# Neighbourhood attention on one core: the denominators' transfers move from SyncE's queue to ScalarE's, the division and the output projection to later tiles, and the queries' split parts to earlier ones

## The reference, cut to what matters

```
x = x + attention(group_norm(x))

qkv = (x @ w_qkv + b_qkv) -> q, k, v        # 16 heads of 8 channels
for each of the 7 x 7 neighbours (a, b) of a position:
    logit = sum_d(q * k[neighbour]) + rpb[head, offset]
attn = softmax over the 49 neighbours
out  = sum over neighbours of attn * v[neighbour]
return out @ w_proj + b_proj
```

## Time and profile before

| | before |
|---|---|
| median of 3 runs | 1369.31 us (1366.49 to 1371.41) |
| profiled execution | 1369.89 us, of which 1368.1 us from the first to the last instruction |
| PE busy | 1142.9 us, 84% of the span |
| DVE busy | 896.4 us, 66% |
| ACT busy | 672.9 us, 49% |
| POOL busy | 580.8 us, 42% |
| mean granted clock of TensorE | 0.868 of full speed |

### The profile page before, as it was taken

The page is one execution under the profiler, slowest core; times in us unless marked ns, Lnnn a source line. Parts: engine busy times, 40 slices in busy tenths (PEclk is TensorE's granted clock), DMA queues, the critical chain, the costliest instruction groups (busy, mean ns, idle before and its releaser), DMA issues.

```text
span 1368.1 us, 33536 instructions
## 1 busy us (share of the span) xinstructions
PE 1142.9 (84%) x12441; PEld 781.8 (57%) x12441; DVE 896.4 (66%) x2136; ACT 672.9 (49%) x1867; POOL 580.8 (42%) x1278
## 2 busy tenths in 40 slices
PE   3799999564889898988889898989888898989883
PEld 3555555362556565655556566656556565656561
DVE  2422222497778686877778686868677686868672
ACT  2200000420657566575657566666656575665761
POOL 3000000410446473746556464737455464637361
PEclk7699999755789899998888999989998888999996
DMA  9200000060574746656574746456565747465562
GB/s 256 57 36 36 36 35 36 24 157 13 120 160 116 147 115 133 149 105 166 118 172 112 163 109 140 130 118 148 116 167 128 158 107 161 112 136 146 105 161 52
DMA packets 142458, 159.17 MB, mean 116 GB/s; under 512 B 29952, under 2 KB 119888, under 8 KB 142040
## 3 DMA queue, kind: packets, MB, share of 16 engines
q1 hardware_dynamic: 141432, 153.13, 48.6%
q0 software_dynamic: 864, 3.90, 0.9%
HBM read 86.09 MB, written 70.47 MB: 114 GB/s over the span
## 4 chain that ended last, share of the span: by engine, by line
PE 50%; DMA 20%; DVE 12%; SPq 9%; issue 6%; ACT 1%; POOL 1%; POOLq 0%; DVEq 0%; ACTq 0%
PE PS L1088 14%; PE PS L1194 9%; DMA area<-q_parts 8%; DMA sums<-packed 8%; PE PS L1157 8%; SPq L436 5%; PE PS L1178 4%; PE PS L1204 4%; PE PS L1100 4%; DVE bias L941 3%; PE PS L1171 3%; PE PS L1141 3%; DVE area L983 3%; DMA area<-x 2%; SPq L488 1%
## 5 line engine op out<-in xcount | busy, mean ns | idle before, releaser
L578 POOL TENSOR_TENSOR halves<-masked 128x96 f32<-128x96 f32 (+1 forms) x512 | 202.8, 396 | 445.7 <-DVE masked L1015 405.9
L1194 PE MATMUL PS<-S,VT 128*36 128x96 f32 (+1 forms) x4096 | 295.2, 270 | 9.9 <-ACT S L761 9.9
L761 ACT ACTIVATE S<-S 128x384 f32<-128x384 f32 (+1 forms) x512 | 270.0, 538 | 64.8 <-DVE S L1004 64.2
L1004 DVE TENSOR_TENSOR S<-PS,bias 128x384 f32<-128x384 f32 (+1 forms) x513 | 283.1, 552 | 7.6 <-PE PS L1157 7.5
L754 ACT ACTIVATE VT<-PS 128x128 f32<-128x128 f32 x449 | 125.9, 280 | 329.2 <-PE PS L1141 323.6
L1157 PE MATMUL PS<-area 97*128 97x48 bf16 (+1 forms) x4112 | 257.1, 210 | 31.7 <-DMA area<-q_parts 22.2
L1194 PEld LDWEIGHTS PS<-S,VT 128*36 128x36 f32 x4096 | 178.5, 120 | 155.1 <-issue 94.5
L1157 PEld LDWEIGHTS PS<-area 97*128 97x128 bf16 x4112 | 185.7, 104 | 118.9 <-DMA area<-q_parts 26.2
L994 DVE TENSOR_REDUCE mcol<-PS 128x6 bf16<-128x480 f32 (+2 forms) x297 | 181.1, 610 | 89.5 <-PE PS L1178 88.0
L1015 DVE TENSOR_TENSOR masked<-PS,cst 128x192 f32<-128x192 f32 (+1 forms) x512 | 181.3, 354 | 85.7 <-PE PS L1194 80.1
L1088 PE MATMUL PS<-area 128*128 128x392 f32 x576 | 192.9, 498 | 3.8 <-DVE area L883 3.8
(11 more groups left out here) (87 smaller groups left out, 1130.2 us busy)
## 6 DMA issues: line engine op xcount, KB each, us to landing
k_parts<-area SPq DMA_DIRECT2D x204, 168.0 KB, 3.0
area<-k_parts SPq DMA_DIRECT2D x33, 1008.0 KB, 7.6
q_parts<-area SPq DMA_DIRECT2D x204, 98.0 KB, 2.2
area<-q_parts SPq DMA_DIRECT2D x66, 294.0 KB, 8.1
xa<-x_mid SPq DMA_DIRECT2D x18, 392.0 KB, 4.8
late<-x_mid SPq DMA_DIRECT2D x17, 392.0 KB, 7.2
out<-area SPq DMA_DIRECT2D x17, 392.0 KB, 6.2
den<-sums SPq DMA_DIRECT2D x66, 98.0 KB
```

The costliest lines, as they stand in the source:

```text
L578: nc.gpsimd.tensor_tensor(h, m[:, :, 0:2, :], m[:, :, 2:4, :], ALU.add).then_inc(s["half"], 1)
L761: nc.scalar.activation(S[:, n % 4, 0:cols], S[:, n % 4, 0:cols], ACT.Exp).then_inc(s["probs"], 1)
L1004: nc.vector.tensor_tensor(S[:, n % 4, 0:cols], PS[:, SCORE + n % 2, 0:cols], bias[:, at:at + cols], ALU.add).then_inc(s["biased"], 1)
L1194: last = mm(PS[64 * (g % 2):64 * (g % 2) + VALUE_COLS, SUM + n % 2, at:at + q], VT[:, w % 4, g, :], S[:, n % 4, q * g:q * (g + 1)], start= ...
```

## The change

Five things are changed, all in the loop.

1. The six transfers of the denominators are issued by ACT, not SP, at fixed steps: `sums<-late` at step 3, `packed<-sums` at step 5, `sums<-packed` at step 8, `den<-sums` at step 11, each at the end of ACT's step with the wait that SP had ahead of it.
2. The reciprocals move from DVE's step 6 to 7, behind that step's maxima, and the division from step 12 to 14.
3. Both halves of the projection are at PE's step 15, one behind the other. ACT keeps the result at step 15 as before.
4. ACT writes the queries' second part at step 11 of the even chunk, not 14. POOL writes their third part at steps 14 and 15, not 17 and 18 (1 and 2 of the odd chunk).
5. SP's queue loses the six transfers and their waits, and keeps the order of the rest.

```diff
-        MISC_PROJECT, MISC_TURN = 13, 24
+        MISC_PROJECT, MISC_TURN = 15, 24
...
-        FIRST_BANK, RECIPROCAL, NORMALIZE, NEXT_IMAGE, RESIDUAL = 1, 6, 12, 30, 20
+        FIRST_BANK, RECIPROCAL, NORMALIZE, NEXT_IMAGE, RESIDUAL = 1, 7, 14, 30, 20
+        COLLECT, PACK, SPREAD_OUT = 3, 5, 11
...
-        SECOND = {8: ("k", 0), 10: ("k", 1), 14: ("q", 0)}
+        SECOND = {8: ("k", 0), 10: ("k", 1), 11: ("q", 0)}
...
-        THIRD = {10: ("k", 0), 11: ("k", 1), 12: ("k", 2), 13: ("k", 3), 17: ("q", 0), 18: ("q", 1)}
+        THIRD = {10: ("k", 0), 11: ("k", 1), 12: ("k", 2), 13: ("k", 3), 14: ("q", 0), 15: ("q", 1)}
...
                         store_keys(j, i + 1, True)
-                        collect_denominators(j, c)
                         store_queries(j, i + 1, True)
                         fill_keys(j, c + 1)
-                        spread_reciprocals(j, c)
                         fill_queries(j, c + 1)
...
+                        if n == COLLECT:
+                            collect_denominators(j, c)
+                        if n == PACK:
+                            pack_denominators(j, c)
+                        if n == RECIPROCAL + 1:
+                            store_reciprocals(j, c)
+                        if n == SPREAD_OUT:
+                            spread_reciprocals(j, c)
...
-                        if MISC_PROJECT <= n < MISC_PROJECT + 2:
-                            project_out(j, c, n - MISC_PROJECT)
+                        if n == MISC_PROJECT:
+                            for g in range(2):
+                                project_out(j, c, g)
```

52 lines of the change are left out of this document (28 added, 24 removed).

## The result

| | before | after |
|---|---|---|
| median of 3 runs | 1369.31 us | 1429.99 us (1429.94 to 1437.98) |
| ratio to before | | 1.0446 (95% interval 1.0415 to 1.0476) |
| span of the profiled execution | 1368.1 us | 1428.2 us |
| PE busy, PE idle (span less busy) | 1142.9, 225.2 us | 1170.4, 257.8 us |
| mean granted clock | 0.868 | 0.865 |

The changed kernel takes 60.7 us more. The two spans differ by 60.1 us: 32.6 us of it is PE standing idle and 27.5 us is PE busy for longer with the same 12441 instructions. Only the first part can be read from waits; the second is taken up under "Open".

What follows compares the result with a forecast made beforehand. PE bounds the kernel, its removable idle time at chunk ends. Per image, 2.9 us even-chunk loss less 2.7 odd-chunk gain plus 1.0 for clock is 1.2, 19 us in 16 images: 1389 us, own range 1374 to 1409, 8 in 10 1340 to 1430.

Steps and rivals of the forecast that it cites:

- PE waits for exponentials, more than before: Before weighing tile 12: PE waits 3.1 us in even chunks and about 0.8 us in odd chunks.
- PE waits for kept values: Odd chunks, step 13: the value ACT keeps is late and holds PE's next turn for another 0.7 us.
- PE waits for the division: At the projection: PE waits 1.3 us in even chunks and 0.9 us in odd chunks.
- PE waits for the queries' load: Odd chunks, before scores: the load's wait of 1.4 us goes, though up to 0.5 us may stay.
- taken for the clock: Three more groups of weighings at 0.86 in place of 0.53 us: 1.0 us per image, bounds 0 and 2.
- the waits of before: PE's removable idle time near chunk ends: 1.5 us per even chunk, 5.1 per odd chunk, 6.6 per image.
- ACT waits for POOL at step 11 of even chunks: ACT waits about 1.4 us for POOL's second difference of the queries before writing their second part.
- the rest of the edits: Issues at steps 3, 5 and 8 and reciprocals at 7 cost nothing; projection's length same; clock 1.0 us per image.
- Rival 2: `den` lands late beside SP's transfers, 5.1 us in place of 3.6: 3.0 us more per image, 1437 us; chance 0.12.
- the doubling: `den` on ACT's queue, served every second turn beside SP's transfers: its moving part would up to double, pointing to 1437 us.
- no projection stands there any more: Even chunks: PE is ready to weigh tile 12 at 743.15, may weigh at 746.2, so waits 3.1 us.
- Rival 1: Issuing from ACT costs it nothing, lying beside running work: -1.5 us per image, 1346 us; chance 0.33.

Runs made afterwards that it cites:

- The run with short keys: Changed kernel with 80 of the 96 rows of the keys' load issued in odd chunks left out: 1410.0 us, ratio 1.027.
- the first experiment: Changed kernel, but SP waits for the packed denominators to land before issuing the next keys' load in odd chunks: 1515.3 us, ratio 1.105.
- all three remedies: Changed kernel with queries' second part at step 14, sums<-late and packed<-sums at steps 2 and 4, den<-sums at 9: 1403.7 us, ratio 1.0221.

## Why the prediction was right in its direction and wrong in its size

I forecast 1389 us, +19 against the profiled execution of before; it was +60.7. Per image of two chunks, by the prediction's own terms (the waits after the loop, 12.9 us in both kernels, left out):

| us per image | forecast | measured |
|---|---|---|
| PE waits for exponentials, more than before | 3.1 + 0.8 = 3.9 | 43.5 / 16 = 2.7 |
| PE waits for kept values | 0.7 | 11.4 / 16 = 0.7 |
| PE waits for the division | 1.3 + 0.9 = 2.2 | (60.0 - 12.9) / 16 = 2.9 |
| PE waits for the queries' load | 0 | 0 |
| PE waits for the bias, more than before | 0 | 40.7 / 16 = 2.5 |
| rest: taken for the clock; measured, PE busy for longer, less 3.9 us of other waits | 1.0 | (60.1 - 36.5) / 16 = 1.5 |
| less the waits of before | 6.6 | 6.6 |
| sum | 1.2 | 3.7 |

Without the line on the bias the measured sum would be the 1.2 us of the forecast. That is in part luck, since the terms are not independent: with the pack a step earlier that line is nearly gone, and the kernel is still 30 us slower than before.

**Right.** SP's wait for `sums<-packed` and PE's for the queries' load went. ACT waits for POOL at step 11 of even chunks: 1.4 us forecast, 1.38 in the row at 770.67. PE's wait for exponentials behind it was put at 3.1 us and is 2.7, in all 16 even chunks. The exponentials of odd chunks, put at 0.8 us, are not late.

**Wrong in kind: issues and reciprocals costed at nothing.** I had written that I am wrong in kind if PE's new idle time lies at steps 3 to 9, and 40.7 us lie there. The step that failed is the one on the rest of the edits: "Issues at steps 3, 5 and 8 [...] lie in steps where ACT waits for PE's turns [...] and I cost them at nothing", with "Reciprocals at step 7 in place of 6 delay one tile's bias in the same way as before: nothing". Of the issues I asked only what they cost ACT; that was right (7.1 us of waits before 16 exponentials in the whole run). I did not ask what is in flight when they are issued. I had counted it a gain that the loads start 5 us earlier, and for `sums<-packed` and `den` I did look for the collision; for `packed<-sums` I did not. With loads that came earlier, it stood behind them at step 5 (8.5 us from its issue's end; before it had in the odd chunk landed within 1.6 us, ahead of the loads: 759.55 to the reciprocals at 761.18), and DVE waits in order, in front of the bias. The run with short keys and the one with the pack a step earlier show the cause: 56.7 us of waits became 13.7 and 12.8. In time this step is worth 28 of the 60.7 us; the 1401.8 us that are left lie within the forecast's own range of 1374 to 1409.

**Wrong in size: how long `den` takes.** I took 3.6 us from the end of issuing to the division's start. In the row at 777.67 it was 777.67 - 772.19 = 5.5 us, and in the odd chunk behind it, issued up to 807.21 and divided at 812.89, 5.7. PE's waits for the division, put at 1.3 us in even and 0.9 in odd chunks, are 1.6 and 1.3. Rival 2 had 5.1 for this and 1437 us for the whole, the nearest of my cases; its mark, a wait for `den` over 4 us in both chunks, did not come, since DVE itself was late (2.57 at 777.67).

For the Trainium skill's rule in "DMA: Bandwidth & Descriptors", "Queues, rings and completion order" (engines take turns between the rings of SP and ACT, packet by packet), 5.5 over 3.6 is within the doubling that I had estimated from it. But the pack went from 1.6 to 8.5 us and `sums<-packed` from 1.5 to 9.5 us in the first experiment, and these are far outside the estimate. The doubling was my own step: taking turns gives it only where the packets of both sides take the same time, and no run looked at packets, so the rule itself is neither borne out nor refuted here. What is measured is that a queue of its own didn't protect a small transfer: `sums<-packed` behind the keys alone in SP's queue took 7.1 us, on ACT's queue behind keys and queries on SP's 9.5.

**Priced nearly right, put down to the wrong edit: the projection's move.** I costed its length and its clock, 1.0 us per image, and let "no projection stands there any more" enter only as the time at which PE is ready. So the 3.1 us were in the sum, but as a price of ACT's order. That half a projection was the work that hid ACT's lateness, I didn't see. The runs show it twice: with the earlier queries alone ACT's wait for POOL is the same 1.4 us and PE's wait 10.3 us; with only the projection later it is 53.8. By itself this is worth 9 us (1339.7 to 1349.0), since the projection then no longer waits. In the kernel before with the queries late it is dearer: together with the division and the reciprocals' step 34 us (ratio 1.025), for the scores at step 14 come ahead of the projection and stand 95.9 us before their load.

**Not asked: the spreading at 11.** I took step 11 as given and asked only for its cost at that place. At step 9 ACT stands up to 7.5 us for the landing, which looks worse and is better: with `SPREAD_OUT = 9` the changed kernel is 35 us faster.

**Rival 1** (issuing from ACT costs nothing, 1346 us) was right in its premise and wrong in its result in this kernel. ACT's waits for issuing are 0.4 us per image, and PE waits 2.7 us for the exponentials all the same. The time that it names is where the transfers on ACT with the old division came out, 1345.2 us, but that is luck: another kernel by another way, not the one worked out.

**Open.** PE is busy 27.5 us longer with the same instructions, nearly half of the loss, and in no experiment was the clock varied by itself. The profiled executions of the other versions show how much of each time is of this kind (us; the granted clock is the mean over 700 to 1300 us):

| version | span | PE busy | PE idle | granted clock |
|---|---|---|---|---|
| before | 1368.1 | 1142.9 | 225.2 | 0.89 |
| before with earlier queries | 1353.3 | 1136.8 | 216.5 | 0.90 |
| the change | 1428.2 | 1170.4 | 257.8 | 0.87 |
| the change, six transfers on SP | 1376.7 | 1137.3 | 239.4 | 0.88 |
| the change, pack at 4 | 1397.0 | 1156.8 | 240.2 | 0.87 |
| the change, spreading at 9 | 1393.3 | 1167.0 | 226.3 | 0.85 |
| the change, all three remedies | 1406.9 | 1174.2 | 232.7 | 0.86 |
| transfers on ACT, old division (1345.2 us) | 1341.5 | 1137.4 | 204.1 | 0.92 |
| division 14, projection 15 (1361.7 us) | 1358.5 | 1140.0 | 218.5 | 0.90 |
| division 12, projection 13 and 14 (1339.7 us) | 1332.7 | 1130.6 | 202.1 | 0.91 |

With the spreading at 9 PE stands idle no longer than before, 1.1 us more, and the kernel is slower by its busy time alone. Of the 64 us between the last version and the one with all three remedies (74 in these two executions), 43.6 are busy time. So the lists of waits explain little more than half of the loss; that the rest is the clock fits the column on the right in the main, but which edit lowers it isn't shown. Over the whole span the means hide it (0.868 and 0.865), since the 345 us before the loop ran at 0.82 before and at 0.87 after. By lines, the weighing is busy 6.9 us longer (295.2 to 302.1) and the projection of the next image's values 7.3 us (29.4 to 36.7).

Nor is it settled how much of the step of 40 us in the table belongs to the reciprocals at 7 alone: both constants changed at once. The version with all three remedies differs from the 1361.7 us one by the reciprocals at 7 and the second part at 14, and is 42 us slower, though the second part at 14 by itself gained 21 in the changed kernel. So the reciprocals at 7 probably cost with the spreading at 9 too. One way is in the trace: ACT then stands 2.5 us for `sums<-packed` in even chunks as well. The share is not measured.

## What to carry to other kernels

When transfers are moved so that a large load starts earlier, list every small transfer that is issued within the load's time, on any queue, and ask which engine waits in order for its landing: the delay goes to whichever is behind, and ordering one ahead hands it to the next. Before work is moved away from a place where an engine waits, ask whose lateness that work hides; a wait before it may be the cheapest place for the wait to be. Change an arrangement of fixed steps one constant at a time: here two of the five parts (the earlier queries, then the transfers on ACT) were worth -16 and -10 us by their ratios, and the rest on top of them cost about 88.

## What the runs showed of the hardware

- **Issuing from ACT runs beside the activations ahead of it, not beside those behind it.** The two `den<-sums` at 770.68 took 1.51 us of ACT's queue, and ACT computed meanwhile what stood ahead of them in its order, a second part and two spreads; the exponentials behind them started at 772.46, after the issues' end at 772.19, and lost nothing. I had taken 0.7 us of 1.36 as lost. Where ACT has to wait for a landing first, nothing is left to compute, and the issues count in full: 762.94 + 1.30 = 764.24 in the first experiment, and exponentials at 764.29. In the changed kernel the waits for issuing are 7.1 us in all, 0.4 us per image. What holds ACT most is the wait ahead of an issue: up to 7.6 us for `sums<-packed` in the version with all three remedies.
- **A small transfer issued behind large ones on the other queue lands late.** Behind keys and queries (1.6 MB) the pack took 8.5 us, `sums<-packed` 9.5 and `den` 9.4, by the rows above. Issued 0.25 us ahead of the keys, the pack was there for the reciprocals 3.3 us after its issue. These are rows of the version of 1345.2 us:

```profile
746.31 0.35 ACTq L769 DMA_DIRECT2D packed<-sums  x1
...
746.56 0.60 SPq L454 DMA_DIRECT2D area<-k_parts  x1
...
749.94 0.47 DVE L1034 RECIPROCAL packed<-packed 128x49 f32<-128x49 f32 x1 [0.83 <-DMA packed<-sums]
```

- **The projection's four matmul records in a row** took 2.98 us in 17 of the 33 chunks of the changed kernel, at a granted clock of 0.50 (778.71 to 781.69), the lower of the two levels of TensorE's clock, and 1.58 us in three, at 1.00 (1075.68 to 1077.26). Split in two halves with other work between, a half of two records took 0.82 to 1.68 us in the version of 1345.2 us.
